# Spreading the second image's routing over six steps of the first image's expert tiles

## The reference, cut to what matters

```python
t = t + attention_linear(layernorm(t))        # 8 heads, keys and queries each through a softmax
xt = layernorm(t)
probs = softmax(xt @ Wr + br)                 # 8 experts
top_p, top_idx = top_k(probs, 2)              # each token goes to two experts
weights = top_p / top_p.sum()
y_e = gelu(ln_e(xt) @ W1[e] + b1[e]) @ W2[e] + b2[e]     # 128 -> 512 -> 128
t = t + weights[0] * y_top0 + weights[1] * y_top1
```

## Time and profile before

| what | value |
|---|---|
| median of three runs | 353.12 us (351.27 to 354.50) |
| profiled execution, its own time | 353.49 us |
| its span on the core | 351.4 us |
| mean granted TensorE clock | 0.956 of full |
| busy PE / DVE / ACT / POOL | 321.8 / 201.8 / 208.8 / 110.7 us |

### The profile page before, as it was taken

The page is one execution under the profiler, slowest core; times in us unless marked ns, Lnnn a source line. Parts: engine busy times, 40 slices in busy tenths (PEclk is TensorE's granted clock), DMA queues, the critical chain, the costliest instruction groups (busy, mean ns, idle before and its releaser), DMA issues.

```text
span 351.4 us, 6589 instructions
## 1 busy us (share of the span) xinstructions
PE 321.8 (92%) x2004; PEld 207.9 (59%) x2004; DVE 201.8 (57%) x616; ACT 208.8 (59%) x328; POOL 110.7 (31%) x140
## 2 busy tenths in 40 slices
PE   7988799999999989999999879697479999999995
PEld 3543444444354435355343336686479999999995
DVE  1477435484756752664757546756836557777610
ACT  1380576877778764545567320647447877778722
POOL 2065094100000001000022781006377777454530
PEclk9996989999999999999999998698969999999999
DMA  6059890887100035000000113001023323223315
GB/s 201 5 106 208 186 208 14 280 233 246 74 2 3 3 92 150 0 2 1 2 0 8 55 46 76 10 8 38 25 76 85 92 85 92 70 71 107 107 65 204
DMA packets 21772, 29.28 MB, mean 83 GB/s; under 512 B 4055, under 2 KB 15628, under 8 KB 21484
## 3 DMA queue, kind: packets, MB, share of 16 engines
q1 hardware_dynamic: 16808, 18.04, 19.5%
q0 software_dynamic: 3744, 10.31, 9.4%
q10 hardware_dynamic: 1188, 0.53, 0.6%
HBM read 11.62 MB, written 9.25 MB: 59 GB/s over the span
## 4 chain that ended last, share of the span: by engine, by line
PE 78%; DVE 10%; POOL 5%; issue 4%; ACT 2%; DVEq 0%; POOLq 0%
PE ps L900 15%; PE ps L1115 12%; PE ps L1102 12%; PE ps L877 9%; PE ps L840 5%; PE ps L858 4%; POOL expert_in L514 4%; PE ps L958 3%; PE ps L735 2%; PE ps L807 2%; PE ps L775 2%; PE ps L1076 1%; DVE pm L1226 1%; PE ps L973 1%; PE ps L1142 1%
## 5 line engine op out<-in xcount | busy, mean ns | idle before, releaser
L581 ACT ACTIVATE probs<-ps 128x1024 f32<-128x1024 f32 x64 | 65.3, 1020 | 27.7 <-PE ps L877 27.6
L900 PE MATMUL ps<-probs,vT 128*32 128x512 f32 x256 | 68.5, 610 | 0.3
L900 PE MATMUL ps<-probs,ones 128*32 128x512 f32 x256 | 68.5, 611 | 0.0
L1115 PE MATMUL ps<-w,GT 128*128 x368 | 51.9, 286 | 5.7 <-ACT GT L713 5.5
L1102 PE MATMUL ps<-XTT,w1s 128*128 128x128 f32 x368 | 51.7, 286 | 4.9 <-issue 4.9
L1223 DVE CUSTOM_DVE_ANT_0 above<-ps,above 128x512 f32<-128x512 f32 x56 | 37.2, 689 | 29.8 <-PE ps L858 28.3
L519 POOL DMA_INDIRECT token_out<-Y,yidx x46 | 44.1, 959 | 31.9 <-DVE Y L1520 26.2
L456 POOL TENSOR_TENSOR rstd<-ve,minus_half 128x1 f32<-128x1 f32 (+2 forms) x6 | 10.4, 1725 | 136.2 <-DVE ve L1271 61.0
L1102 PEld LDWEIGHTS ps<-XTT,w1s 128*128 128x128 f32 x368 | 47.5, 202 | 6.1 <-issue 6.1
L1115 PEld LDWEIGHTS ps<-w,GT 128*128 128x128 f32 x368 | 46.8, 199 | 7.2 <-issue 7.0
L713 ACT ACTIVATE GT<-H 128x512 f32<-128x512 f32 x46 | 29.0, 630 | 28.5 <-DVE H L1509 28.4
(11 more groups left out here) (199 smaller groups left out, 432.0 us busy)
## 6 DMA issues: line engine op xcount, KB each, us to landing
expert_in<-zeros POOLq DMA_DIRECT2D x2, 1495.0 KB, 10.3
XR<-expert_in SPq DMA_DIRECT2D x46, 65.0 KB, 1.9
Qs<-q_hi SPq DMA_DIRECT2D x16, 128.0 KB, 3.4
w<-in_L_ffn_W SPq DMA_DIRECT2D x1, 2048.0 KB, 8.4
w<-in_L_ffn_W SPq DMA_DIRECT2D x8, 256.0 KB, 4.3
YG<-token_out SPq DMA_DIRECT2D x8, 256.0 KB, 4.2
Ks<-k_hi SPq DMA_DIRECT2D x14, 128.0 KB, 3.5
X<-in_x SPq DMA_DIRECT2D x2, 512.0 KB, 4.6
```

The lines of the kernel that those rows point to most:

```text
L581: nc.scalar.activation(probs[:, s % 3, :], bank(2 + 2 * (s % 2), 2), ACT.Exp).then_inc(exp_done, 1)
L900: last = nc.tensor.matmul(bank(acc_bank(o))[i * HD:(i + 1) * HD, :], w, probs[:, s % 3, hd * HALF:(hd + 1) * HALF], start=kt == 0, stop=kt ...
L1115: last = nc.tensor.matmul(bank(4 + p)[:, 0:D], GT[:, p, c, :], w2[:, e, c, :], start=c == 0, stop=c == HC - 1)
```

## The change

The pieces of image 1 that follow its logits are cut smaller and moved back in the tables. `v_route` is cut into "route" and "weights"; `v_slots` into "counts", "places" (slots), "tables" and "affine". On DVE the logits go from behind step 2 to behind step 4, and the pieces lie behind steps 4, 5, 6, 7, 8, 9 and 10, one tile's H and Y between any two. On PE the counting product goes from the middle of step 5 to the middle of step 7. On ACT the Exp goes from step 2 to step 4, and the four norm pieces from steps 3 and 4 to 5 and 6. PE's logits stay at step 2. For image 0 the new names stand side by side, so its instructions and their order are as before. No instruction is added or removed.

```diff
-                     53: "gates_exp", 54: "route choose norm2_0", 55: "norm2_1", 56: "norm2_2 counts", 57: "norm2_3"}
-        LAYER1_PE = {"before": "residual project query_value0 query_value1 keys", 0: "keyT", "1 mid": "context queryT fold",
-                     1: "attend", "2 mid": "tokenT", 2: "logits", "5 mid": "counts"}
-        LAYER1_DVE = {"before": "tokens_stats tokens query_value0 query_value1 query_max keys",
-                      0: "queries queries_scaled", "1 mid": "context fold", 1: "attend stats",
-                      2: "logits shift", 3: "route choose", 4: "counts"}
-        LAYER1_ACT = {"before": "tokens_stats", "first": "queries_exp keys_exp keyT_sb", "1 mid": "queryT_sb",
-                      "2 mid": "tokenT_sb", 2: "gates_exp", 3: "norm2_0 norm2_1", 4: "norm2_2 norm2_3"}
+                     53: "gates_exp", 54: "route weights choose norm2_0", 55: "norm2_1", 56: "norm2_2 counts places tables affine", 57: "norm2_3"}
+        LAYER1_PE = {'before': 'residual project query_value0 query_value1 keys', '1 mid': 'context queryT fold', 1: 'attend', '2 mid': 'tokenT', 2: 'logits', '7 mid': 'counts', 0: 'keyT'}
+        LAYER1_DVE = {'before': 'tokens_stats tokens query_value0 query_value1 query_max keys', 0: 'queries queries_scaled', '1 mid': 'context fold', 1: 'attend stats', 4: 'logits shift', 5: 'route', 6: 'weights choose', 7: 'counts', 8: 'places', 9: 'tables', 10: 'affine'}
+        LAYER1_ACT = {'before': 'tokens_stats', 'first': 'queries_exp keys_exp keyT_sb', '1 mid': 'queryT_sb', '2 mid': 'tokenT_sb', 4: 'gates_exp', 5: 'norm2_0 norm2_1', 6: 'norm2_2 norm2_3'}
...
                 link(last)
+
+            def v_weights(b):
                 nc.vector.tensor_copy(topf[:, :, :], topi[:, :, 0:2])
...
                 link(nc.vector.tensor_tensor(cnt[:, 2, :], cnt[:, 1, :], cnt[:, 0, :], ALU.subtract))
+
+            def v_places(b):
                 link(nc.vector.tensor_tensor(slotv, slotv,
...
+            def v_tables(b):
                 link(nc.vector.tensor_tensor(cmp, t_iota[:, :, :],
...
+
+            def v_affine(b):
                 link(nc.vector.tensor_tensor(cmp, iota_e[:, :].unsqueeze(1).broadcast_to([P, TILES, E]),
...
-                      "counts": [v_slots]}
+                      "counts": [v_slots], "places": [v_places], "tables": [v_tables],
+                      "affine": [v_affine], "weights": [v_weights]}
```

## The result

The changed kernel takes 348.59 us (median of 6 runs, 347.72 to 349.88), the kernel before 353.67 us (median of 6). The ratio is 0.987, with a 95% interval of 0.9841 to 0.9898: faster by 1.0 to 1.6%. Forecast were 348.7 us and 1.2%. Executions over 1.5% above the fastest of the same kernel are left out of every ratio and interval here, but not of the medians.

What follows compares the result with a forecast made beforehand. PE bounds the kernel, losing 14.9 us over nine tiles to stalls behind DVE's blocks and a low clock. Profiled 353.49 less 4.4 gives 349.1, or 348.7 us against the median (1.2% less); range 344.8 to 352.8.

Steps and rivals of the forecast that it cites:

- DVE is the bound of steps 4 to 10: Seven steps need 22.4 us on DVE against 13.3 at the steady 1.90 a tile; spreading hides only PE's and ACT's needs.
- handover: DVE idle behind a piece before the next H: 0.48 to 0.61 us, taken as 0.52, paid seven times instead of three.
- The sum: DVE's 22.4 us plus waits takes H(4) at 241.4 to H(11) at 265.2; second product 11 at 266.7, gain 4.4 us.
- The stalls forecast for PE: ACT's Exp, table loads and norm pieces, 6.5 us, make PE stand 0.8 us at 245.0, 0.6 at 247.1, 1.6 at 248.9.
- the wait at Y(6): DVE waits about 0.9 us for Y(6) because of ACT, all that leaks through of ACT's delays.
- The clock: PE at 2.4 GHz throughout steps 4 to 10, as all stalls there are under 1.7 us.
- Rival (b): PE's clock falls once under frequent short stalls, costing about 4 us of PE work, half covered: 350.7 us; chance 0.13.
- Scatter and sends: Scatter(1) starts 6.6 us later, tile 23 arrives with 1.7 to spare, POOL catches up about when tiles end: no cost.
- rival (c): Tile 23's transpose waits for the late scatter; gain gone from start 265.1, over 1% slower past 268.6; chance 0.08.
- Rival (d): DVE's idle ahead of H behind pieces shrinks to nothing, gaining 3.5 us more: 345.2 us; chance 0.12.
- Rival (a): The work only moves its stall: DVE's work unchanged, ACT's 3.2 us wholly uncovered, 351.9 us; chance 0.14.
- (e): ACT's table switches between gelu(4) and gelu(5) show a drain of 2.8 us once not hidden: 351.5 us; chance 0.03.

Runs made afterwards that it cites:

- best2: Changed kernel with early register read, ACT's norm pieces spread, eight sends before the scatter, and PE's counting product behind step 7: 344.80 us, ratio 0.9743.
- norm_spread: Changed kernel with ACT's norm pieces behind steps 6, 7 (two) and 8 instead of 5 and 6: median 350.52 us, ratio 0.9858.
- no_switch: Changed kernel with image 1's Exp of the router logits replaced by a copy, so ACT switches no function table: 348.99 us, ratio 0.9883.
- split_only: Kernel before with the pieces cut as in the change but two steps earlier, so without the shift: median 351.13 us, ratio 0.9898.
- early_reg: Changed kernel with DVE's register read of the next tile's expert right behind H instead of ahead of the next H: 346.13 us, ratio 0.9797.
- early_sent8: Changed kernel with DVE's early register read and eight sends instead of four ahead of the scatter: 347.48 us, ratio 0.981.
- best: Changed kernel with DVE's early register read, ACT's norm pieces spread and eight sends instead of four ahead of the scatter: 347.78 us, ratio 0.9812.
- later4: Changed kernel with every piece behind the logits product another four steps later: 358.7 us, ratio 1.0114.
- the shift alone: Kernel before with image 1's pieces two tiles later but as coarse as before: 350.98 us, ratio 0.9942.
- a clock kept up alone: Kernel before with identity matmuls whose result nobody reads in its two long PE stalls: 350.65 us, ratio 0.9888.

## Why the prediction was right

By its own steps:

- **DVE is the bound of steps 4 to 10.** Shown: DVE is busy or in its handover from H(4) to H(11) but for 0.18 us at Y(3) and 0.80 at Y(6); taking 2.56 us of table loads from ACT did not move H(7), taking the handover away moved second product 11 by 3.1.
- **The sum.** H(4) to H(11) was 23.8 forecast, 23.8 measured; the stretch gained 4.6, forecast 4.4. Three terms inside were off against each other, so the closeness is partly luck: the handover was taken at 0.52 and measured 0.66 on average (4.6 in seven steps, forecast 3.6); the waits for Y were taken at 1.4 and measured 1.0; and DVE's own work was taken at 18.7 (11.6 for the pieces, 7 x 1.02 for H and Y) and measured 18.2, mostly because a piece starts about 0.08 before Y has ended, which the sum counted twice. H(4) itself came 2.19 after second product 2, forecast 2.4. That the time as a whole came within 0.1 us of 348.7 is luck too: the medians differ by 5.1 us, not 4.4, and the kernel before stood at 353.67 with three more runs, not at 353.12.
- **ACT.** The stalls forecast for PE (0.8, 0.6, 1.6) came as 1.14, 0.74, 1.21. The next copy began at once behind the Exp (0.39 forecast), and no drain showed. But the reason given for the wait at Y(6), ACT, was half of it. Second product 6 is queued behind PE's counting product, which starts at 249.29: PE is free for it at 249.28, which is ACT's doing, but DVE has ended the mask only at 249.24. So with ACT's switch gone second product 6 starts no earlier (12.58 against 12.53 us after second product 2), and `best2`, which moves the counting product, shows the gain. "PE's counting product stands behind tile 7's hidden product" was seen, that second product 6 stands behind the counting product was not.
- **The clock.** Right for both profiles of the changed kernel, but the reason, that short stalls are harmless, fell. `norm_spread`, with no stall over 1.14 in this stretch until then, had a granted clock of 0.53 behind one of 0.74, and `no_switch` 0.62 (window 249.4 to 252.9) behind one of 1.58, while `split_only` stayed fast behind 2.38. From second product 2 to 11 the clock was 1.00 in six profiles (the changed kernel twice, `early_reg`, `early_sent8`, `best`, `best2`) and 0.94 in three (`norm_spread`, `no_switch`, `split_only`), so that the changed kernel kept it was in part luck. Rival (b) is no rival but something that comes in some executions. It cost 1.0 us in `no_switch`, where DVE waited for the slow second product 6, and about 0.1 in `split_only`, where DVE set the pace. This fits the Trainium skill, "TensorE: Matmul & The Clock Gate", section "A second HAM failure mode: psum-queue depth-cycling", on frequent short idles, which the prediction had weighed against one row. What decides it in an execution stays open.
- **Scatter and sends.** Tile 23 was in time; POOL caught up at 324.66, and no Y waited for a send. `later4` shows the limit where rival (c) put it, with 5.28 us of wait; that rival was priced without the slow matmuls behind the wait, so it decides sooner than at the start of 268.6 that it gave: `later4`'s scatter started 28.1 after its second product 2, which would be 267.1 in the kernel before, and it was slower than that by 1.1%.
- **Rival (d)**, no handover, did not come by itself, but its bound was sound: 3.5 given, 3.1 measured once the read was moved.
- **Rival (a)** falls with `no_switch`, **(e)** with the row of gelu(5) right behind the load (243.62 + 1.28 = 244.90, gelu at 244.91).

How the 4.6 us divide is not additive: in the traces the shift alone brings 2.5, the cuts alone 2.3, a clock kept up alone 2.7. Each removes part of the same slow matmuls.

## What to carry to other kernels

Cut a long chained block so that every consumer queued behind it gets its turn between two pieces, and count what each cut costs: here 0.66 us of handover, a register read that could be issued behind the previous long instruction for next to nothing. A stall on TensorE has a second price, the slow matmuls behind it. Look at the duration of equal groups behind a stall, not only at the idle time, and then ask whether TensorE is what the next step waits for: behind the stall of 4.59 us the slow matmuls cost 2.7 us, behind that of 2.38 and in `split_only` next to nothing, since VectorE set the pace. Ask what else is queued behind a small product that waits (second product 6 behind the counts), since taking work off an engine that another one covers (ACT here) gains nothing.

## What the runs showed that was not expected

- The same code at the same place took 3.72 or 5.41 us (16 matmuls of image 1's queries and values) in different executions; that alone is 1.7 us of 350.
- The same stall of 0.74 us ahead of the same eight matmuls was followed by 1.15 in both profiles of the changed kernel and by 1.88 in `norm_spread`, whose code up to there is the same.
- Idle matmuls whose result is never read made the kernel 0.6 to 1.7% faster.
